# Layer-wide transformer kernel: other PSUM bank counts for head outputs and filling units, and a reordered filling plan

## The chip, the cores and the metric

One Trainium2 chip, one of its cores, one launch. The metric is the device time of a launch in microseconds, here the median of three runs. A profiled execution of the same kernel has its own time, given beside the others below.

## The reference

Two attention layers over a batch of 8 sequences of 512 rows by 512 columns, 16 heads of 32 columns each. All is fp32.

```python
def layer0(tgt, memory, Wq, Wk, Wv):               # x, ctx_1024: (8, 512, 512)
    q, k, v = heads(tgt @ Wq.T), heads(memory @ Wk.T), heads(memory @ Wv.T)
    att = softmax(q k^T / sqrt(32)) v
    return tgt + att[0]                            # sequence 0's attention, added to all eight

def layer1(x, y, ...):                             # x is layer0's result, y is ctx_1024 again
    xq, ykv = layer_norm(x, gq, bq), layer_norm(y, gkv, bkv)
    q = heads(xq @ Wq); k, v = heads(ykv @ Wkv)
    x = x + concat(softmax(q k^T * 32**-0.5) v) @ Wproj + bproj
    h = gelu(layer_norm(x, gm, bm) @ W1 + b1)      # 512 -> 2048, exact gelu
    return x + h @ W2 + b2                         # 2048 -> 512
```

Layer 0's attention is needed for sequence 0 alone. So the kernel runs nine attentions: number 0 is layer 0 on sequence 0, numbers 1 to 8 are layer 1 on the eight sequences.

## The kernel before

**Units and ticks.** Every product is done on a pair of fp32r halves (high, and the remainder, low), three matmuls for a product, so that the result keeps fp32's accuracy. The program is laid out by hand in 621 ticks (class `Plan`, from L46). A tick of an attention holds its core work: one matmul of scores `S` (L925, `ps_s`, for the row maximum), one of scores turned round `t` (L940, `ps_t`, seven ticks later, for the exponentials) and two that weigh values `O` (L908, `ps_o`, nine ticks later). Four ticks make a head, 64 an attention. Around the core lie filling units, which use the banks `ps_d`: `k`, `q`, `v` (projections), `out` (Wproj), `hid` (W1) and `y2` (W2), each 12 matmuls of 512 columns in 4 parts of 3, and the transposes `a` (normed ctx or x), `tg` (layer 0's output) and `ht` (normed h), each 4 transposes of 128x128 in one part.

**Where a unit lands.** `spread` lays a list of units over a run of ticks, evenly by cost (12 for a matmul unit, 2 for a transpose unit). A tick has three places: 0 behind `S`, 1 behind `t`, 2 behind the first `O` pairs; with `front=True` all goes to place 0. PE runs all of it in one order. Attention 0 (ticks 4 to 77) is filled with the projections of sequences 1 to 6 (`early`, `keys_values(b)`), then comes a gap of 8 ticks without core work (`late`, transposes of layer 0's output), then attentions 1 to 8. Attention 1, and the first third of attention 2, are filled with `queries` (units `q` and `a` in turn). Attentions 2 to 8 are filled with the previous sequence's `out`, `ht`, `hid` and `y2` units; the tail (`if tail`) does the last sequence without core work.

**Banks and evacuation.** `bank(u)` (L529) gives unit number i bank i % 3 of `ps_d`, and PE waits before its first matmul until unit i - 3 is evacuated (L820). A unit is evacuated in the order of the plan (`EVACUATED`): for `k`, `q`, `v` ScalarE writes the high half (L955), VectorE the low one (L1109); for `a` and `ht` ScalarE applies gain and bias twice (L959, L960), then VectorE subtracts (L1109); `out`, `y2` and `hid` take one VectorE instruction (L1136, L1146, L1139), `tg` two (L1130, L1131). A unit that ends at place 0 is evacuated behind the tick's row maximum and ahead of its exponentials; one that ends at place 1 behind the tick's exponentials (and, on ScalarE, behind the head's `o_raw` copy); one that ends at place 2 at the next tick's start. ScalarE's and VectorE's queues are in that order too, with the core's exponentials (two a tick, L1054 and L1061), row maxima (L1212), `p_lo` (L1225), norms (L1159, L1016) and inverses (L1174 to L1185) in them.

**Heads' outputs.** The four `O` pairs of a head add up in one bank `ps_o`. ScalarE copies it out (`move_head`, L1005, `o_raw`), and the next head's first `O` waits for that copy (L900).

**Weight pieces.** GpSimd splits W1 and W2 into halves in 16 pieces (`piece`, L1258 and L1260, `piece_tick` at L330), between its own `p_lo` work (L1324). SyncE loads a piece two ticks ahead of it and stores it one tick behind it, in the same queue that loads heads and row maxima.

Of the kernel before, what the change touches and what calls it, by code (L numbers as in the profile page):

```python
# [5 lines left out]
F32 = mybir.dt.float32  # L6
F32R = mybir.dt.float32r
ACT = mybir.ActivationFunctionType
# [3 lines left out]
P = 128  # L12
T = 512
D = 512
F = 2048
B = 8
NH = 16
DK = D // NH
FC = D // P
TC = T // P  # L20
HC = F // P
G = P // DK
# [5 lines left out]
VW = 2 * DK + 1  # L28
# [23 lines left out]
PRE = 4  # L52
# [8 lines left out]
class Plan:  # L61
# [42 lines left out]
    def build(self):  # L104
        spread = self.spread
        for t, units in enumerate(([("k", 0, 0)], [("q", 0, 0)], [("v", 0, 0), ("v", 0, 1)],
                                   [("v", 0, 2), ("v", 0, 3)])):
            spread([t], units, front=True)

        t0 = PRE  # L110
        self.core(0, CH, t0)
        spread(range(t0, t0 + 9), [(kind, 0, g) for g in range(1, G) for kind in "kq"])

        def keys_values(b):
            units = []
            for c in range(4):
                units += [("k", b + 1, c), ("v", b + 1, c)]
                if b + 1 < B:
                    units.append(("a", 3 + b, c))
            return units  # L120

        early = [("a", 2, c) for c in range(FC)]
        for b in range(6):
            early += keys_values(b)
        drained = t0 + CH + WEIGH
        spread(range(t0 + 9, drained), early)
        late = keys_values(6) + keys_values(7)

        gap = drained
        first = [("a", 10, c) for c in range(FC)]  # L130
        for i, units in enumerate(([("tg", 0, g) for g in range(G - 1)] + late[:2], late[2:6], [("tg", 0, G - 1)],
                                   late[6:11], late[11:14],
                                   [u for pair in zip(first, late[14:18]) for u in pair], [("q", 1, 0)],
                                   late[18:] + [("q", 1, 1), ("q", 1, 2)])):
            spread([gap + i], units, front=True)
        self.gap = gap

        self.base = {n: gap + 8 + (n - 1) * CH for n in range(1, NP + 1)}
        self.core(CH, NP * CH, self.base[1])
        queries = [("q", 1, 3)] + [("a", 11, c) for c in range(FC)]  # L140
        for n in range(2, NP):
            for g in range(G):
                queries.append(("q", n, g))
                if n + 1 < NP:
                    queries.append(("a", 10 + n, g))
        base = self.base
        spread(range(base[1], base[2] + 15), queries[:-6])

        def second(n, group):
            return [("y2", n, 4 * group + t) for t in range(TC)]  # L150

        def hidden(n, group):
            return [("hid", n, 4 * group + c) for c in range(4)]

        def burst(tick, n, group, units):
            self.bursts.setdefault(tick, []).append((n, group))
            spread([tick], units, front=True)

        def by_chunk(tick, n, group):
            self.by_chunk.setdefault(tick, []).append((n, group))  # L160

        for n in range(2, NP + 1):
            at, old, new = base[n], n - 2, n - 1
            tail = n == NP
            outs = [("out", new, t) for t in range(TC)]
            turns = [("ht", new, c) for c in range(FC)]
            if tail:
                spread([at + 5], second(old, 1)[:2], front=True)
                spread([at + 6], second(old, 1)[2:], front=True)
                burst(at + 7, old, 2, hidden(old, 3))  # L170
                drain = at + WEIGH
                spread([drain - 1], second(old, 2)[:2], behind=True)
                by_chunk(drain - 1, old, 3)
                spread([drain + 1], second(old, 2)[2:], front=True)
                spread([drain + 2], second(old, 3)[:1], front=True)
                spread([drain + 3], outs, front=True)
                spread([drain + 4], second(old, 3)[1:3], front=True)
                spread([drain + 5], turns[:2] + second(old, 3)[3:] + turns[2:], front=True)
                spread([drain + 6], hidden(new, 0), front=True)
                by_chunk(drain + 6, new, 0)  # L180
                spread([drain + 7], hidden(new, 1), front=True)
                by_chunk(drain + 7, new, 1)
                spread([drain + 8], second(new, 0), front=True)
                spread([drain + 9], hidden(new, 2), front=True)
                by_chunk(drain + 9, new, 2)
                spread([drain + 10], second(new, 1), front=True)
                spread([drain + 11], hidden(new, 3), front=True)
                by_chunk(drain + 11, new, 3)
                spread([drain + 12], second(new, 2), front=True)
                spread([drain + 13], second(new, 3), front=True)  # L190
                self.ticks = drain + 15
                continue
            if old:
                burst(at + 5, old, 2, second(old, 1)[:2])
                spread(range(at + 6, at + 15), second(old, 1)[2:] + hidden(old, 3)[:3])
                spread(range(at + 15, at + 22), outs)
                spread(range(at + 22, at + 24), hidden(old, 3)[3:])
                burst(at + 24, old, 3, second(old, 2)[:2])
                rest = second(old, 2)[2:]
                spread(range(at + 25, at + 40), rest + turns + hidden(new, 0))  # L200
                burst(at + 40, new, 0, second(old, 3)[:2])
                spread(range(at + 41, at + 55), second(old, 3)[2:] + hidden(new, 1))
            else:
                spread(range(at + 15, at + 22), outs)
                spread(range(at + 22, at + 35), queries[-6:])
                spread(range(at + 35, at + 48), turns + hidden(new, 0))
                burst(at + 48, new, 0, hidden(new, 1)[:2])
                spread(range(at + 49, at + 55), hidden(new, 1)[2:])
            burst(at + 55, new, 1, second(new, 0)[:2])
            spread(range(at + 56, at + CH + 5), second(new, 0)[2:] + hidden(new, 2))  # L210
# [5 lines left out]
PLAN = Plan()  # L216
NO = PLAN.no
# [109 lines left out]
PIECES = 16  # L327


def piece_tick(i):  # L330
    return PRE + 19 + 5 * i if i < PIECES // 2 else PLAN.gap - 11 + 2 * (i - PIECES // 2)


PIECE_SPLIT = listed([(piece_tick(i), i) for i in range(PIECES)])
# [88 lines left out]
def xattn_program(nc, x, ctx, x0t, ctx0t, l0wq, l0wk, l0wv, wq, wk, wv, wo, w1, w2, cols, bproj, b2, ident, out):  # L423
# [22 lines left out]
    v_s = sb("v_s", [P, 2, TC, G, VW], F32R)  # L446
# [7 lines left out]
    o_raw = sb("o_raw", [P, 2, T], F32)  # L454
# [68 lines left out]

    ps_s = nc.alloc_psum_tensor("ps_s", [P, 2, T], F32)
    ps_t = nc.alloc_psum_tensor("ps_t", [P, 2, T], F32)
    ps_o = nc.alloc_psum_tensor("ps_o", [P, T], F32)
    ps_d = nc.alloc_psum_tensor("ps_d", [P, 3, T], F32)

    def bank(u):  # L529
        return ps_d[:, NO[u] % 3]  # L530

    sem = nc.alloc_semaphore

# [24 lines left out]
    evacuated = sem("evacuated")  # L558
# [17 lines left out]
    o_moved = sem("o_moved")  # L576
# [235 lines left out]
    def _(pe):  # L812
# [4 lines left out]

        def part(kind, n, c, i):
            u = (kind, n, c)
            if i == 0 and NO[u] >= 3:  # L820
                pe.wait_ge(evacuated, NO[u] - 2)
            if kind == "a":
                if n == 10:
                    src = xt0
                else:
                    src = stage[:, (STAGE_NO["y", n - 2] if n < 10 else STAGE_NO["x", n - 10]) % 2]
# [68 lines left out]
        def values(s):  # L895
            h, c = divmod(s, TC)
            group = h // G
            if c == 0:
                if h:
                    pe.wait_ge(o_moved, h)  # L900
                if h % G == 0:
                    pe.wait_ge(v_loaded[group % 2], 16 * (group // 2 + 1))
            if c in POOL_CHUNKS:
                pe.wait_ge(p_pool_split, by_gpsimd(s))
            else:
                pe.wait_ge(p_split, by_vector(s))
            for m, src in enumerate((p_hi, p_lo)):
                ins = nc.tensor.matmul(ps_o[0:VW], v_s[:, group % 2, c, h % G], src[:, c],  # L908
                                       start=(c == 0 and m == 0), stop=(c == TC - 1 and m == 1))
            ins.then_inc(pv_done, 1)  # L910

# [40 lines left out]
    def _(act):  # L952
# [48 lines left out]
        def move_head(h):  # L1001
            act.wait_ge(pv_done, h * TC + TC)
            if h >= 2:
                act.wait_ge(o_placed[(h - 2) % G], ((h - 2) // G + 1) * (16 * PLACE_DMAS))
            act.activation(o_raw[0:VW, h % 2], ps_o[0:VW], ACT.Identity).then_inc(o_moved, 1)  # L1005

        def scaled(kind, i, t):
            no = NORM_NO[kind, i]
# [26 lines left out]
        for tick in range(TICKS):  # L1035
# [11 lines left out]
            if s is not None:  # L1047
                c = s % TC
# [367 lines left out]
```

## Time and profile before

| | us |
|---|---|
| median of 3 runs | 1790.82 (1788.2 to 1792.63) |
| profiled execution | 1793.32 |
| its span, first to last instruction | 1791.5 |
| PE busy in the span | 1714.7 |
| ACT, DVE, POOL busy | 1156.1, 1082.1, 939.3 |
| mean granted TensorE clock | 0.991 of full speed |

PE is TensorE's matmuls and PEld its weight loads; DVE is VectorE, ACT ScalarE, POOL GpSimd, SP SyncE; a q behind an engine's name is its sequencer, which issues DMAs. Matmuls are pipelined, so PE counts as busy while matmuls follow each other; a wait shorter than a matmul's own latency hardly shows as idle time, and is read from the start times. The profiled execution is 2.5 us (0.14%) above the median of the runs, 1.8 us of it outside the span.

### The profile page before, as it was taken

How to read it: one execution, taken by the hardware profiler on the slowest of the kernel's cores; microseconds unless marked ns; L12 is line 12 of the kernel's file. 1: busy time of each engine (PE TensorE's matmuls, PEld its weight loads, DVE VectorE, ACT ScalarE, POOL GpSimd, SP SyncE). 2: the span in 40 equal slices, each digit the busy share in tenths (PEclk: the TensorE clock that was granted, in tenths of full speed). 3: DMA queues.
4: the chain of work that ended last, by engine and by line, in shares of the span. 5: the costliest groups of instructions: out<-in, count | busy, mean ns of one | idle time of the engine just before them, and what ended most of it. 6: DMA issues, size and time to landing. Idle time of an engine off the chain costs nothing.

```text
span 1791.5 us, 23794 instructions
## 1 busy us (share of the span) xinstructions
PE 1714.7 (96%) x7456; PEld 1313.6 (73%) x7456; DVE 1082.1 (60%) x1865; ACT 1156.1 (65%) x1940; POOL 939.3 (52%) x802
## 2 busy tenths in 40 slices
PE   7899998998989999999999999999999999999999
PEld 5677776765666777777777777777777777777787
DVE  5565654477776666665666665666656666654322
ACT  4777764587877765765766577657657665775231
POOL 0444455157675564656465564646664655646341
PEclk9999999999999999999999999999999999999999
DMA  8789978674545675676676566756766775668262
GB/s 285 251 278 302 330 275 322 229 213 164 188 132 162 184 201 138 179 235 162 160 219 195 143 168 185 200 133 179 235 168 157 219 197 142 171 185 274 93 234 79
DMA packets 160077, 356.78 MB, mean 199 GB/s; under 512 B 29392, under 2 KB 50000, under 8 KB 159312
## 3 DMA queue, kind: packets, MB, share of 16 engines
q1 hardware_dynamic: 109072, 189.31, 35.8%
q10 hardware_dynamic: 50880, 165.95, 29.5%
q8 instruction: 61, 1.00, 0.2%
q14 instruction: 64, 0.52, 0.1%
HBM read 253.61 MB, written 82.08 MB: 187 GB/s over the span
## 4 chain that ended last, share of the span: by engine, by line
PE 69%; ACT 8%; DMA 7%; DVE 5%; issue 4%; POOL 3%; SPq 2%; ACTq 0%; DVEq 0%; POOLq 0%
PE ps_d L887 46%; PE ps_o L908 11%; PE ps_t L940 6%; PE ps_s L925 5%; DMA q_st<-negmax_t 3%; ACT p_hi L1054 2%; DVE negmax L1212 1%; DMA rs<-o_raw 1%; ACT ps_d L960 1%; ACT ps_t L1061 1%; ACT ht L1016 1%; POOL p_lo L1324 1%; SPq L728 1%; PE ps_d L815 1%; DMA v_scratch<-v_out 1%
## 5 line engine op out<-in xcount | busy, mean ns | idle before, releaser
L1324 POOL TENSOR_TENSOR p_lo<-p_full,p_hi 128x512 fp32r<-128x512 f32 x288 | 372.1, 1292 | 586.5 <-ACT p_full L1061 586.0
L1054 ACT ACTIVATE p_hi<-ps_t 128x512 fp32r<-128x512 f32 x576 | 345.7, 600 | 358.5 <-PE ps_t L940 355.0
L1212 DVE TENSOR_REDUCE negmax<-ps_s 128x1 fp32r<-128x512 f32 x576 | 388.9, 679 | 128.2 <-PE ps_s L925 127.6
L887 PE MATMUL ps_d<-hT,w_r 128*128 128x512 f32 x1536 | 419.0, 393 | 2.0 <-DVE hT L1109 2.0
L887 PE MATMUL ps_d<-w_r,g_s 128*128 128x512 f32 x1536 | 389.4, 393 | 0.0
L887 PEld LDWEIGHTS ps_d<-hT,w_r 128*128 128x128 f32 x1536 | 288.6, 189 | 73.7 <-DVE hT L1109 5.7
L887 PEld LDWEIGHTS ps_d<-w_r,g_s 128*128 128x128 f32 x1536 | 290.3, 189 | 64.6
L1225 DVE TENSOR_TENSOR p_lo<-ps_t,p_hi 128x512 fp32r<-128x512 f32 x288 | 198.8, 690 | 229.9 <-ACT ps_t L1061 229.2
L908 PE MATMUL ps_o<-p_hi,v_s 128*65 128x512 f32 x576 | 231.5, 402 | 14.7 <-POOL p_lo L1324 8.1
L940 PE MATMUL ps_t<-q_st,k_st 97*128 97x512 f32 x576 | 232.2, 403 | 11.6 <-DMA q_st<-negmax_t 10.9
L925 PE MATMUL ps_s<-k_st,q_st 96*128 96x512 f32 x576 | 231.8, 402 | 8.4 <-DVE negmax L1212 6.6
L908 PE MATMUL ps_o<-p_lo,v_s 128*65 128x512 f32 x576 | 227.4, 395 | 0.0
L1332 POOL TENSOR_TENSOR g_s<-h_st,g_s 128x512 fp32r<-128x512 f32 x128 | 166.2, 1309 | 74.7 <-ACT g_s L1072 74.6
L1061 ACT ACTIVATE ps_t<-ps_t 128x512 f32<-128x512 f32 x288 | 172.8, 600 | 0.0
L1061 ACT ACTIVATE p_full<-ps_t 128x512 f32<-128x512 f32 x288 | 172.1, 598 | 0.0
L925 PEld LDWEIGHTS ps_s<-k_st,q_st 96*128 96x128 f32 x576 | 109.1, 189 | 55.2 <-DVE negmax L1212 12.6
L940 PEld LDWEIGHTS ps_t<-q_st,k_st 97*128 97x128 f32 x576 | 109.0, 189 | 43.4 <-DMA q_st<-negmax_t 18.8
L1139 DVE TENSOR_SCALAR h_st<-ps_d,col_s 128x512 f32<-128x512 f32 x128 | 94.3, 736 | 43.2 <-PE ps_d L887 42.5
L908 PEld LDWEIGHTS ps_o<-p_hi,v_s 128*65 128x65 f32 x576 | 78.5, 136 | 56.8 <-ACT o_raw L1005 13.1
L887 PE MATMUL ps_d<-aT,wk_s 128*128 128x512 f32 x384 | 107.6, 407 | 8.2 <-DVE aT L1109 6.7
L908 PEld LDWEIGHTS ps_o<-p_lo,v_s 128*65 128x65 f32 x576 | 78.7, 137 | 48.2 <-issue 0.6
L887 PE MATMUL ps_d<-aT,wq_s 128*128 128x512 f32 x384 | 110.9, 402 | 0.0
(102 smaller groups left out, 2160.6 us busy)
## 6 DMA issues: line engine op xcount, KB each, us to landing
w_r<-w_scratch ACTq DMA_DIRECT2D x214, 512.0 KB, 5.3
w_r<-w_scratch SPq DMA_DIRECT2D x42, 512.0 KB, 4.7
v_scratch<-v_out SPq DMA_DIRECT2D x36, 520.0 KB, 5.2
k_scratch<-kq_out SPq DMA_DIRECT2D x36, 512.0 KB, 4.9
q_st<-q_scratch SPq DMA_DIRECT2D x144, 128.0 KB, 4.5
k_st<-k_scratch SPq DMA_DIRECT2D x144, 128.0 KB, 4.3
o_ab<-o_raw SPq DMA_DIRECT2D x144, 128.0 KB, 3.5
w_scratch<-piece_out SPq DMA_DIRECT2D x16, 1024.0 KB, 6.4
```

Source lines behind the costliest of these rows:

```text
L728: sp.dma_start(q_st[KQ:KM, h % G, c * P:c * P + P].bitcast(F32), negmax_t[c:P:32, h % 2]).then_inc(row_loaded[h % 2], 16)
L887: ins = nc.tensor.matmul(bank(u), lhs[a], rhs[b], start=(i == 0 and m == 0), stop=(i == 3 and m == 2))
L908: ins = nc.tensor.matmul(ps_o[0:VW], v_s[:, group % 2, c, h % G], src[:, c], start=(c == 0 and m == 0), stop=(c == TC - 1 and m == 1))
L925: nc.tensor.matmul(ps_s[:, c % 2], q_st[0:KQ, h % G, c * P:c * P + P], k_st[0:KQ, h % G], start=True, stop=True).then_inc(s_ready, 1)
L940: nc.tensor.matmul(ps_t[:, c % 2], k_st[0:KM, h % G, c * P:c * P + P], q_st[0:KM, h % G], start=True, stop=True).then_inc(t_ready, 1)
L1054: act.activation(p_hi[:, c], ps_t[:, c % 2], ACT.Exp, scale=SCALE)
L1061: act.activation(whole, ps_t[:, c % 2], ACT.Exp, scale=SCALE).then_inc(p_exp, 1)
L1139: dve.tensor_scalar(hidden_of(n, c // 4)[:, c % 4], bank(u), col_s[:, 6 * FC + c:6 * FC + c + 1], None, ALU.add).then_inc(evacuated, 1)
L1212: dve.tensor_reduce(negmax[:, h % 2, c:c + 1], ps_s[:, c % 2], AX.X, ALU.max, negate=True).then_inc(s_maxed, 1)
L1225: dve.tensor_tensor(p_lo[:, c], ps_t[:, c % 2], p_hi[:, c].bitcast(F32), ALU.subtract).then_inc(p_split, 1)
L1324: pool.tensor_tensor(p_lo[:, c], p_full[:, (by_gpsimd(s) - 1) % 2], p_hi[:, c].bitcast(F32), ALU.subtract).then_inc(p_pool_split, 1)
L1332: pool.tensor_tensor(g_s[:, done % 2, 1, c], hidden_of(n, group)[:, c], g_s[:, done % 2, 0, c].bitcast(F32), ALU.subtract).then_inc(g_lo, 1)
```

## The change

Five edits. The two PSUM ones go together, since PSUM has eight banks and the kernel uses all of them.

- `ps_o` has two banks, used by heads in turn; a head's first `O` waits for the copy of the head before the previous one. `ps_d` has two banks in place of three; a unit waits for the evacuation of the unit two before it.
- `keys_values`: the order of a sequence's units. Before: k0 v0 a0 k1 v1 a1 k2 v2 a2 k3 v3 a3. After: k0 v0 a0 k1 a1 v1 a2 k2 a3 v2 k3 v3 (`a` of the next sequence). The lists `early` and `late` are made of it, the latter cut at the same places.
- Attentions 3 to 8: the last two `y2` units of group 2 get ticks 25 to 27 of the attention for themselves, and the `ht` and `hid` units behind them ticks 28 to 39; before, all shared ticks 25 to 39.
- Tail: the last `y2` unit of the seventh sequence's group 3 comes ahead of the four `ht` units; before, it stood behind the second of them.
- W2's pieces (8 to 15) come six ticks earlier: ticks 60, 62, ... 74 in place of 66 to 80.

```diff
         def keys_values(b):
             units = []
-            for c in range(4):
-                units += [("k", b + 1, c), ("v", b + 1, c)]
-                if b + 1 < B:
-                    units.append(("a", 3 + b, c))
+            turns = [("a", 3 + b, c) for c in range(FC) if b + 1 < B]
+            units = [("k", b + 1, 0), ("v", b + 1, 0), *turns[:1], ("k", b + 1, 1), *turns[1:2], ("v", b + 1, 1), *turns[2:3],
+                     ("k", b + 1, 2), *turns[3:], ("v", b + 1, 2), ("k", b + 1, 3), ("v", b + 1, 3)]
             return units
...
-                spread([drain + 4], second(old, 3)[1:3], front=True)
-                spread([drain + 5], turns[:2] + second(old, 3)[3:] + turns[2:], front=True)
+                spread([drain + 4], second(old, 3)[1:], front=True)
+                spread([drain + 5], turns, front=True)
...
-                spread(range(at + 25, at + 40), rest + turns + hidden(new, 0))
+                spread(range(at + 25, at + 28), rest)
+                spread(range(at + 28, at + 40), turns + hidden(new, 0))
...
 def piece_tick(i):
-    return PRE + 19 + 5 * i if i < PIECES // 2 else PLAN.gap - 11 + 2 * (i - PIECES // 2)
+    return PRE + 19 + 5 * i if i < PIECES // 2 else PLAN.gap - 17 + 2 * (i - PIECES // 2)
...
-    ps_o = nc.alloc_psum_tensor("ps_o", [P, T], F32)
-    ps_d = nc.alloc_psum_tensor("ps_d", [P, 3, T], F32)
+    ps_o = nc.alloc_psum_tensor("ps_o", [P, 2, T], F32)
+    ps_d = nc.alloc_psum_tensor("ps_d", [P, 2, T], F32)
 
     def bank(u):
-        return ps_d[:, NO[u] % 3]
+        return ps_d[:, NO[u] % 2]
...
-            if i == 0 and NO[u] >= 3:
-                pe.wait_ge(evacuated, NO[u] - 2)
+            if i == 0 and NO[u] >= 2:
+                pe.wait_ge(evacuated, NO[u] - 1)
...
             if c == 0:
-                if h:
-                    pe.wait_ge(o_moved, h)
+                if h >= 2:
+                    pe.wait_ge(o_moved, h - 1)
...
-                ins = nc.tensor.matmul(ps_o[0:VW], v_s[:, group % 2, c, h % G], src[:, c],
+                ins = nc.tensor.matmul(ps_o[0:VW, h % 2], v_s[:, group % 2, c, h % G], src[:, c],
...
-            act.activation(o_raw[0:VW, h % 2], ps_o[0:VW], ACT.Identity).then_inc(o_moved, 1)
+            act.activation(o_raw[0:VW, h % 2], ps_o[0:VW, h % 2], ACT.Identity).then_inc(o_moved, 1)
```

## Rows read from the trace of the kernel before

**Rows 1.** The page: shares of the span of the chain that ended last, by engine.
```profile
PE 69%; ACT 8%; DMA 7%; DVE 5%; issue 4%; POOL 3%; SPq 2%; ACTq 0%; DVEq 0%; POOLq 0%
```

**Rows 2.** Busy time by stretch: stretch, length, engines with instruction counts, clock, DMA, GB/s.
```profile
130.00:200.00 70.00, 68.19 (x312) 53.48 (x311) 48.56 (x88) 50.20 (x88) 36.84 (x32) 1.00 0.96 319
...
343.00:420.00 77.00, 64.23 (x280) 45.31 (x278) 54.54 (x104) 60.84 (x107) 43.54 (x45) 0.98 0.67 215
420.00:490.00 70.00, 64.49 (x273) 46.39 (x274) 52.06 (x97) 58.87 (x108) 41.39 (x39) 0.95 0.54 174
490.00:560.00 70.00, 64.43 (x281) 46.71 (x279) 49.69 (x93) 52.15 (x96) 43.70 (x42) 1.00 0.38 121
641.00:806.00 165.00, 162.63 (x707) 124.42 (x706) 103.59 (x176) 110.84 (x186) 93.25 (x76) 1.00 0.64 180
```

**Rows 3.** The waits, whole span: who waited for whom, total us, times, longest.
```profile
PEld ps_o L908 <- ACT o_raw L1005: 13.1, 28, 1.3
...
PE ps_o L908 <- ACT o_raw L1005: 4.1, 8, 0.9
```

**Rows 4.** Timeline, attention 0, first v-a-k: start, length, engine, line, what, [idle before].
```profile
72.53 0.84 PE L887 MATMUL ps_d<-wv_s,aT 128*128 128x512 f32 x3
...
73.45 0.60 PE L815 MATMUL ps_d<-id_s,stage 128*128 128x128 f32 x4
73.47 0.65 ACT L955 ACTIVATE v_out<-ps_d 128x512 fp32r<-128x512 f32 x1 [2.21 <-PE ps_d L887]
...
73.81 1.63 PE L887 MATMUL ps_d<-aT,wk_s 128*128 128x512 f32 x6
...
74.16 0.69 DVE L1109 TENSOR_TENSOR v_out<-ps_d,v_out 128x512 fp32r<-128x512 f32 x1 [0.73 <-ACT v_out L955]
```

**Rows 5.** Timeline, attention 0, one of its last v-a-k.
```profile
245.70 0.94 PE L887 MATMUL ps_d<-aT,wk_s 128*128 128x512 f32 x3
...
246.30 0.69 DVE L1109 TENSOR_TENSOR v_out<-ps_d,v_out 128x512 fp32r<-128x512 f32 x1 [0.34 <-ACT v_out L955]
```

**Rows 6.** Timeline, the gap: ScalarE's norm, the last transpose's evacuation, PE.
```profile
305.55 1.50 ACT L1016 ACTIVATE xt<-xt,shift,rstd 128x512 f32<-128x512 f32 x2
...
306.95 0.76 ACT L959 ACTIVATE aT<-ps_d,col_s 128x512 fp32r<-128x512 f32 x1
...
309.37 1.65 PE L887 MATMUL ps_d<-aT,wk_s 128*128 128x512 f32 x3 [3.36 <-DVE aT L1109]
```

**Rows 7.** Timeline, PE near attention 0's end.
```profile
262.00 0.42 PE L908 MATMUL ps_o<-p_hi,v_s 128*65 128x512 f32 x1 [2.27 <-POOL p_lo L1324]
```

**Rows 8.** Timeline, attention 1, first q-a-q.
```profile
358.72 0.69 DVE L1109 TENSOR_TENSOR kq_out<-ps_d,kq_out 128x512 fp32r<-128x512 f32 x1 [0.43 <-ACT kq_out L955]
358.74 0.86 PE L887 MATMUL ps_d<-aT,wq_s 128*128 128x512 f32 x3
```

**Rows 9.** Timeline, attention 3, from the last y2 unit to hid.
```profile
719.16 0.85 PE L887 MATMUL ps_d<-w_r,g_s 128*128 128x512 f32 x3
...
720.09 0.60 PE L815 MATMUL ps_d<-id_s,ht 128*128 128x128 f32 x4
...
722.82 0.68 DVE L1146 TENSOR_TENSOR xres_b<-ps_d,xres_b 128x512 f32<-128x512 f32 x1
...
723.55 0.66 PE L815 MATMUL ps_d<-id_s,ht 128*128 128x128 f32 x4 [1.25 <-DVE xres_b L1146]
```

**Rows 10.** Timeline, tail: the last four transpose units.
```profile
1693.61 1.31 PE L815 MATMUL ps_d<-id_s,ht 128*128 128x128 f32 x8 [3.05 <-ACT ht L1016]
...
1694.57 4.45 PE L887 MATMUL ps_d<-w_r,g_s 128*128 128x512 f32 x12
```

**Rows 11.** Busy time by stretch, around falls of the clock (columns as in rows 2).
```profile
308.50:315.30 6.80, 5.93 (x14) 4.67 (x15) 1.51 (x3) 0.60 (x1) 0.00 (x0) 0.50 0.41 165
421.10:424.50 3.40, 3.40 (x9) 2.42 (x8) 2.04 (x4) 2.72 (x5) 1.27 (x1) 0.50 0.72 233
411.70:421.10 9.40, 6.74 (x27) 4.38 (x28) 5.31 (x10) 6.38 (x12) 8.38 (x11) 1.00 0.48 175
```

## The prediction

> **What bounds the kernel now.** Read first the shares of the chain that ended last: PE holds 69% of it, and no other engine more than 8% [rows 1]. So the kernel is priced in PE's time, and what matters elsewhere is what makes PE wait. Then the busy times by stretch: in attention 0 and in the steady attentions PE is busy 97 to 99% of the time, 68.2 of 70 us and 162.6 of 165 us; in attention 1 and the start of attention 2 it idles 12.8, 5.5 and 5.6 us, 24 us in all [rows 2]. So a new wait on PE adds whole in the first kind of stretch, and in the second it can take the place of waits that are there. Then the waits: the copy of a head's output holds PE up 4.1 us in 8 places, and its weight loads 13.1 us in 28 [rows 3]. Last the timeline, at the places where a fourth unit now finds a third bank and will not after the change.
>
> **Two banks in place of three, attention 0.** A unit must then wait until the unit two before it is evacuated. Between them lies one unit. Where that is 12 matmuls, it is about 2.8 us of PE (a part of three takes 0.7 us by its start times), and the cover is enough. Where it is a transpose unit, its four transposes take 0.36 us: from 73.45 to the next part at 73.81 [rows 4]. The evacuation of a `v` is ScalarE's 0.65 us and, behind it, VectorE's 0.69 us, and the trace has its end at 74.85; the `k` two units on starts at 73.81 [rows 4]. In the changed kernel both have one bank, and PE waits the 1.04 us. One of the last such triples: end 246.99, start 245.70, short by 1.29 us [rows 5]. Attention 0 has 23 such triples v-a-k, and each is short, by 0.27 to 1.83 us, 1.07 us on average. The new order of `keys_values` doesn't take them away. It makes them, in each sequence, v0-a0-k1, k1-a1-v1, v1-a2-k2 and k2-a3-v2: four for four. A `k` is evacuated by the same two instructions as a `v`. So 6 sequences x 4 x 1.07 = **+25.7 us**. The four transpose units in a row at its start already wait for banks; with one bank fewer I estimate +2.5 (0 to 4). The bounds of the 25.7 are 17, if every evacuation ran at its shortest with no work ahead of it in the queues, and 31.
>
> **The new order's gain.** What it does remove is the wait of the next sequence's first `k` for the last transpose unit. In the gap ScalarE has two more norm instructions ahead of that evacuation (1.50 us), it starts at 306.95, and PE idles 3.36 us [rows 6]; the clock then stands at 0.50 for 6.8 us [rows 11], in which half the work is lost, 3.4 us. After the change two to three units lie between, at 2.8 us each. **-6.8 us** in the gap, and -3.0 for two smaller cases of the kind in attention 0.
>
> **The gap's own bank waits.** Eight triples with an `a` in the middle remain there, with no core work to lengthen them: 1.25 us each, the size of the second one above [rows 5], and 0.8 of it waited already: **+9.5**. The transposes of layer 0's output wait for banks before and after; I put nothing. The gap comes to +2.7, with -1 to +10 as bounds.
>
> **Pieces six ticks earlier.** GpSimd's pieces near the end of attention 0 make its `p_lo` late, and PE waits 2.27 us for one [rows 7]. In SyncE's queue each piece's load and store now pass six ticks of heads, row maxima and stores, in a stretch just behind one with a DMA share of 0.96 [rows 2]. The same crowding can come six ticks sooner, so I take -1.5 out of -3 to +2.
>
> **Attentions 1 and 2: q-a-q.** A `q` ends its evacuation at 359.41, and the `q` two units on starts at 358.74: short by 0.67 us [rows 8]. Of 23 such triples 19 are short, by 0.2 to 3.7 us, 20.5 us in all; the long ones are those that end behind the tick's exponentials. With four `a` in a row at the head (+2) and the first `ht` (+2) that is 24.5 us. But here PE idles 24 us already, some 17 of it for row maxima, GpSimd and DMA, work that goes on while PE waits for a bank. I take half of the 17 as absorbed: **+16.5**, between 8 (all of it) and 24 (none).
>
> **Heads' outputs.** The wait that the second bank removes is 4.1 us by PE's idle time, and at most 13.1 by its weight loads', which overlap matmuls [rows 3]. **-5**, being nearer to the idle time.
>
> The Trainium skill, Perfetto Trace Analysis, section Matmuls, asks that independent groups of matmuls rotate through different banks so that one's evacuation overlaps the next one's matmuls. It holds for both rotations alike, and by it the change would only gain: the first rival below. The rows agree with it for groups of 12 matmuls alone, and not for those of four transposes.
>
> **ht units, six steady attentions.** Before, PE idles 1.25 us at the third `ht`, which waits for the last `y2` unit's addition: that ends at 723.50, and the transposes start at 723.55 [rows 9]. The new ticks bring that `y2` unit's end ahead of the first `ht` by a tick's core work, but with two banks the second `ht` needs it, and its addition is still queued behind the next row maximum: 1.2 us. The fourth `ht` needs the second one's evacuation, which on ScalarE stands behind two exponentials and an `o_raw` copy, 1.8 us, then takes two instructions of about 0.75 (one such in [rows 6]) and VectorE's 0.7: about 4.1 us, against 1.6 us of PE work between: 2.5. The third `ht` and the first `hid` add 0.6. That is 4.3 against 1.25, so +3.0, six times **+18** (9 to 25).
>
> **Tail.** PE idles 3.05 us ahead of the first `ht`, and the 12 matmuls of the `y2` unit stand behind it and take 4.45 us where 12 otherwise take 2.8 [rows 10]. Moved ahead, they fill the idle time. But the four `ht` units then have nothing between them and two banks: each from the second on waits for the `y2` unit's or an earlier `ht`'s evacuation, 0.5, 2, 1.3 and, for the first `hid`, 1.3 us. I put **0** (-2 to +3).
>
> **Clock.** It fell to half for 3.4 us behind a stretch of 9.4 us with PE busy for 6.74 [rows 11]. New waits of 1 us every 3 to 8 us are sparser than that, but in attention 1 they join waits that are there. I add two to three falls of 1.7 us each: **+4** (0 to 15).
>
> **Sum.** 25.7 + 2.5 - 3.0 + 2.7 - 1.5 + 16.5 - 5 + 18 + 0 + 4 = +59.9. The profiled execution would go from 1793.3 to 1853.2; it stands 2.5 us above the median of the runs, and the sum is put on that: 1790.8 + 60 = **1851 us**, 3.3% slower. The low ends of the terms together give +12, the high ends +107; they are independent enough that I take 1815 to 1890 for this case.
>
> **Rivals.**
> - *The waits are covered, and the kernel is faster.* If evacuations kept ahead of PE with two banks, the gains would stand alone: 13.1 at most for heads' outputs, 9.8 for the order, 3 for pieces and 3 in the tail: 1790.8 - 29 = 1762, or about 1775 with half of them. It decides at about 25 us of bank waits: below that the change is faster. Against it speak the ends and starts in rows 4, 5 and 8, of instructions that need one bank after the change. 4%; no difference, 2%.
> - *Half is absorbed everywhere.* PE's waits let ScalarE's and VectorE's queues run dry, so evacuations come at their shortest, and core waits vanish: 17 + 0 + 8 + 9 less the gains of 15 or so gives +20: 1811. For it: PE's idle time in attention 1 [rows 2]. Against it: PE has next to no idle time elsewhere. 14%.
> - *The clock.* Waits join to stretches like that in rows 11, and 20 more falls come, most in attentions 0 and 1: 20 x 1.7 = 34 in place of 4: 1881. For it: one fall in attention 1 came from small waits alone. Against it: in attention 0 most new waits stand alone. 10%.
>
> **Chances.** The forecast 70%, the others as above. A measurement of this kernel can tell about 0.3%, 5.4 us, from no change: faster 0.04, the same 0.02, slower 0.94. The range, which holds what lies between the second rival and the third, is 1815 to 1890.
>
> **What would show it.** In the profile after: PE waits at L887 and L815 for L1109, about 1 us each, in some 24 places in attention 0 and 8 in the gap; four small waits at the `ht` units of each steady attention in place of one; none at `ps_o` for `o_raw`; no wait of 3.36 us in the gap. A steady attention would grow from 164 us by about 3. It would be wrong if the waits for L1109 summed to under 30 us, or if another engine's work behind these waits came later than I count it.

## The result, and the profile after

The change makes the kernel slower: 1858.4 us against 1791.7, a ratio of 1.035 (95% interval 1.033 to 1.037), +63 us by the ratio. The span of the profiled execution goes from 1791.5 to 1855.7 us. The forecast was 1851, +60.

The waits of PE in the changed kernel, whole span (who waited for whom: total us, times, longest):

```profile
PE ps_d L887 <- DVE kq_out L1109: 32.8, 30, 3.6
PE ps_d L887 <- DVE v_out L1109: 18.8, 17, 2.5
PE ps_d L815 <- DVE hT L1109: 17.3, 15, 1.9
PE ps_d L815 <- DVE kq_out L1109: 9.2, 3, 7.2
...
PE ps_o L908 <- POOL p_lo L1324: 1.6, 2, 0.9
```

Four rows of waits for banks hold 78 us. The row of heads' outputs waiting for `o_raw`, 4.1 us of PE's idle time before [rows 3], is gone from the list. All four were ended by the low half's instruction on VectorE (L1109), the last step of an evacuation.

Busy time by stretch, for the stretches that answer to [rows 2], and two in which the clock stood at half (columns: length, then PE, PEld, DVE, ACT, POOL, each with its instruction count, granted clock, DMA share, GB/s):

```profile
130.00:200.00 70.00, 61.91 (x277) 47.14 (x276) 41.62 (x77) 45.19 (x79) 29.91 (x27) 1.00 0.78 259
376.00:453.00 77.00, 61.74 (x258) 45.34 (x258) 53.82 (x101) 56.70 (x99) 38.99 (x41) 0.92 0.64 201
453.00:528.00 75.00, 67.49 (x293) 48.86 (x293) 53.99 (x100) 63.82 (x115) 45.89 (x44) 0.97 0.56 176
682.00:850.00 168.00, 164.95 (x707) 126.34 (x707) 104.71 (x176) 111.27 (x186) 93.30 (x76) 0.98 0.64 178
764.40:771.20 6.80, 5.64 (x15) 4.00 (x16) 4.35 (x8) 5.62 (x10) 5.05 (x4) 0.50 0.58 200
...
61.20:74.80 13.60, 9.19 (x26) 6.62 (x27) 4.06 (x6) 10.27 (x16) 6.24 (x5) 0.50 0.10 43
```

In the same 70 us of attention 0 PE starts 277 matmuls where it started 312 [rows 2]; a steady attention's 707 matmuls take 168 us where they took 165. In attention 0 the clock is full in that stretch, so what is missing there is waits alone. In the steady attention the clock has fallen to half for 6.8 us, which it didn't do before.

The first v-a-k triple of the changed kernel, on the timeline (start, length, engine, line, operation, tiles, idle time before), answers to [rows 4]:

```profile
79.76 0.84 PE L887 MATMUL ps_d<-wv_s,aT 128*128 128x512 f32 x3
...
80.67 0.60 PE L815 MATMUL ps_d<-id_s,stage 128*128 128x128 f32 x4
80.70 0.64 ACT L955 ACTIVATE v_out<-ps_d 128x512 fp32r<-128x512 f32 x1 [2.20 <-PE ps_d L887]
...
81.37 0.69 DVE L1109 TENSOR_TENSOR v_out<-ps_d,v_out 128x512 fp32r<-128x512 f32 x1 [0.72 <-ACT v_out L955]
...
82.11 1.20 PE L887 MATMUL ps_d<-aT,wk_s 128*128 128x512 f32 x4 [0.84 <-DVE v_out L1109]
```

The transposes start at 80.67 and the `k` could follow 0.36 us later, at 81.03; the `v` unit's evacuation ends at 82.06 and the `k` starts at 82.11. The engines' own durations are as before. The idle time shown, 0.84, is shorter than the loss by start times, 1.08, since the last transpose still counts as busy.

Stretch by stretch, from the start times of PE's matmuls, in us. A matmul at full clock counts 0.231 and a transpose 0.109, their usual distance from start to start; what the falls of the clock cost is at most that much again for each one that starts in them; the waits at units are those ahead of a unit's first instruction; the rest is core waits and waits inside a unit, such as the 3.36 us of [rows 6].

| stretch | forecast | longer by | waits at units | clock | rest |
|---|---|---|---|---|---|
| start and attention 0 | +23.7 | +30.0 | +37.8 | +3.8 | -11.5 |
| gap | +2.7 | +2.6 | +8.3 | -2.8 | -2.9 |
| attentions 1 and 2 | +11.5 | +8.4 | +25.3 | +3.6 | -20.5 |
| attentions 3 to 8 | +18 | +22.3 | +12.9 | +11.4 | -2.0 |
| tail | 0 | +0.8 | +0.7 | +1.2 | -1.1 |
| clock, all | +4 | | | +17.2 | |
| sum | +59.9 | +64.1 | +85.0 | +17.2 | -38.1 |

The same start times say which units wait. Where 12 matmuls stand between a unit and the one two before it, 5 of 394 units start more than 0.3 us late, and all 394 together 7.7 us; in the kernel before it was 4, and 7.4 us. Where four transposes stand between, 84 of 100 do, 109.5 us together; before it was 17, and 25.8 us. So nearly all the new waits at units are behind transpose units.

### The profile page after: what moved, and what is told of

It reads as the page before. It is cut to its first block, busy times and chain, and to the rows that moved or that the text cites. A ratio compares the mean times of both kernels' runs of the same rounds, so it can differ in the third digit from the quotient of the medians.

```text
span 1855.7 us, 23794 instructions
## 1 busy us (share of the span) xinstructions
PE 1736.8 (94%) x7456; PEld 1329.2 (72%) x7456; DVE 1088.8 (59%) x1865; ACT 1160.4 (63%) x1940; POOL 939.3 (51%) x802
## 4 chain that ended last, share of the span: by engine, by line
PE 75%; DVE 7%; DMA 6%; ACT 5%; issue 2%; SPq 2%; POOL 2%; DVEq 0%; ACTq 0%; POOLq 0%
PE ps_d L887 51%; PE ps_o L908 12%; PE ps_t L940 6%; PE ps_s L925 6%; DMA q_st<-negmax_t 2%; DMA rs<-o_raw 2%; DVE negmax L1212 1%; DVE kq_out L1109 1%; DVE stats L1159 1%; SPq L728 1%; ACT ps_d L960 1%; ACT p_hi L1054 1%; SPq L723 1%; ACT ps_t L1061 1%; PE ps_d L815 1%
## 5 line engine op out<-in xcount | busy, mean ns | idle before, releaser
L887 PE MATMUL ps_d<-hT,w_r 128*128 128x512 f32 x1536 | 427.9, 399 | 2.2 <-DVE hT L1109 2.0
L887 PEld LDWEIGHTS ps_d<-hT,w_r 128*128 128x128 f32 x1536 | 294.7, 192 | 76.9 <-DVE hT L1109 6.5
L887 PE MATMUL ps_d<-aT,wq_s 128*128 128x512 f32 x384 | 115.0, 414 | 21.0 <-DVE kq_out L1109 19.7
L887 PE MATMUL ps_d<-wv_s,aT 128*128 128x512 f32 x384 | 103.4, 396 | 13.3 <-DVE kq_out L1109 13.1
```

The source lines that it names most:

```text
L887: ins = nc.tensor.matmul(bank(u), lhs[a], rhs[b], start=(i == 0 and m == 0), stop=(i == 3 and m == 2))
```

## The experiments

The theory: PE waits for banks behind units of four transposes, because an evacuation lasts longer than they do, and with two banks nothing else lies between. The rivals: the moved work costs the time; the clock does; the evacuating engines' rate does. Times are differences by the ratio to the kernel before on the same chip, with the ratio's interval.

**The order edits without the PSUM edits.** The changed kernel with

```diff
-    ps_o = nc.alloc_psum_tensor("ps_o", [P, 2, T], F32)
-    ps_d = nc.alloc_psum_tensor("ps_d", [P, 2, T], F32)
+    ps_o = nc.alloc_psum_tensor("ps_o", [P, T], F32)
+    ps_d = nc.alloc_psum_tensor("ps_d", [P, 3, T], F32)
...
-                pe.wait_ge(evacuated, NO[u] - 1)
+                pe.wait_ge(evacuated, NO[u] - 2)
...
-                    pe.wait_ge(o_moved, h - 1)
+                    pe.wait_ge(o_moved, h)
```

> All of the change but the PSUM edits: the new order of the filling units, the new ticks for ht, the new tail, the early pieces, with one bank for heads' outputs and three for the units as before. My theory, that the time is lost to bank waits behind transpose units: without them the order's gains stand alone, 6.8 in the gap, 3 in attention 0, 1.5 for pieces, up to 3 in the tail, so about 1791 - 12 = 1779 us. The rival, that the moved work itself costs the time (the transposes in a row in the tail, the pieces beside more DMAs, the ht ticks): 1815 us or more.

Measured: +2.1 us (-0.9 to +5.0), 1794.7. The moved work does not cost the time: the first rival is out. But the gain of 12 isn't there either. The waits of PE in this kernel say where part of it went:

```profile
PE ps_d L887 <- DVE hT L1109: 9.0, 9, 1.4
...
PE ps_d L815 <- ACT stage L1016: 4.6, 3, 3.3
...
PE ps_d L815 <- DVE hT L1109: 3.8, 7, 1.4
```

The steady attentions are 8.7 us longer than before (waits behind the `ht` units in more places, three falls of the clock), and the transposes `a` of sequence 7 wait 3.3 us for their norm. The gap is 4.3 us shorter and the tail 2.7.

**The PSUM edits without the order edits.** The kernel before with

```diff
-    ps_o = nc.alloc_psum_tensor("ps_o", [P, T], F32)
-    ps_d = nc.alloc_psum_tensor("ps_d", [P, 3, T], F32)
+    ps_o = nc.alloc_psum_tensor("ps_o", [P, 2, T], F32)
+    ps_d = nc.alloc_psum_tensor("ps_d", [P, 2, T], F32)
...
-                pe.wait_ge(evacuated, NO[u] - 2)
+                pe.wait_ge(evacuated, NO[u] - 1)
...
-                    pe.wait_ge(o_moved, h)
+                    pe.wait_ge(o_moved, h - 1)
```

> The PSUM edits alone on the kernel before: two banks for heads' outputs, two for the units, the old order. My theory: the whole cost of the change and none of its order's gain, 1858 + 10 = about 1868 us, with waits for evacuations at the k behind each transpose unit, and with waits for a last transpose unit still there. The rival, that the order costs the time: within 10 us of the kernel before.

Measured: +65 us (61 to 70), 1859.9. This is the whole cost, in the old order. The order's gain of 10 is missing here as well: 1859.9 against 1858.4. In the profiles the new order has the shorter gap and tail, by 4.5 and 4.3 us, and the longer attention 0 and attentions 3 to 8, by 6.6 and 3.2.

**The wait alone, with three banks there.**

```diff
-                pe.wait_ge(evacuated, NO[u] - 2)
+                pe.wait_ge(evacuated, NO[u] - 1)
```

> The kernel before with nothing changed but the wait: each unit waits for the evacuation of the unit two before it, as if there were two banks; three are there, and heads' outputs have one. Beside the kernel with the PSUM edits alone in the old order this prices the second bank for heads' outputs. My theory: 5 us slower than that one (between 4 and 13), about 1873 us. The rival, that waits for banks take the place of the waits for o_raw: the same within 2 us, since PE's other waits give the copy its time.

Measured: +67 us (64 to 71), 1861.5. Nothing else differs from the kernel before, so a wait for the evacuation of the unit two before is enough to make the loss. The second bank for heads' outputs is worth 1.6 us beside it, within what these runs can tell from nothing, and not 5. The rival of this run came out: where PE waits for banks, the copy has its time anyway; the row of waits for `o_raw` is gone from this kernel's list too, with one bank.

**The a units' transposes twice, in the changed kernel.**

```diff
-            for t in range(TC):
+            for t in [*range(TC)] * (2 if u[0] == "a" else 1):
```

> The changed kernel with the four transposes of each of the 64 units a done twice into the same bank: 256 more transposes of about 0.11 us, 28 us more of PE's work. My theory, that PE waits behind these units because they are too short to cover an evacuation: the work goes into waits that are there already, and the time rises by less than 8 us, or falls if fewer falls of the clock come: 1850 to 1866 us. The rival, that the evacuations' own rate sets the waits (a longer unit only ends later, and so does its evacuation): 1858 + 28 = 1886 us.

Measured: +56 us (51 to 61), 1852.1: 6 us faster than the changed kernel, with 256 transposes more. Its waits:

```profile
PE ps_d L887 <- DVE kq_out L1109: 19.0, 23, 3.1
PE ps_d L815 <- DVE hT L1109: 17.3, 15, 1.9
PE ps_d L887 <- DVE v_out L1109: 12.9, 15, 2.5
```

The waits for `k`, `q` and `v` units fall from 32.8 and 18.8 us to 19.0 and 12.9, and those at `ht` units, which were left as they were, stay at 17.3. From a unit `a`'s first transpose to the next matmul, without a wait, PE now takes 0.79 us in the median, where it took 0.36: 64 x 0.43 = 27.6 us of work. By start times the waits at units fall by 25.2 us. So the work goes into the waits, as the theory has it. Had the evacuating engines' rate set the waits, they would have moved along with the longer units, and the time would have grown by 28.

**The same doubling in the kernel before.** The same line.

> The kernel before with the four transposes of each of the 64 units a done twice: the same 256 extra transposes as in the changed kernel with doubled transposes, which became 6 us faster by them. My theory: here there are few waits for them to fill, so 28 us of work, less what attention 1's idle time takes up, +20 (14 to 28), about 1813 us. The rival, that a doubled transpose costs PE little in any kernel (then the other run showed nothing): under +8 us.

Measured: +5.4 us (1.8 to 9.1), 1800.0. This expectation missed, and the rival's number came out, though not for its reason: the transposes take their 0.43 us each here too. By start times the core's waits fall by 15.8 us, the clock's falls by 3.3 and waits at units by 3.2. So the kernel before had some 16 us of core waits that other work can fill, 5 of them in attention 0, where I had counted on none. The two runs differ in where the work goes: in the changed kernel waits at units fall by 25.2 us and the rest by some 4, here by 3.2 and 15.8.

**The wait in one stretch at a time.** The kernel before with the stricter wait under a condition on the tick at which a unit starts:

```diff
-                pe.wait_ge(evacuated, NO[u] - 2)
+                pe.wait_ge(evacuated, NO[u] - (1 if PLAN.starts[u] < PLAN.gap else 2))
```

> The kernel before, three banks and its old order, with the stricter wait (the unit two before) only for units that start in attention 0 and ahead of it. It prices the term of attention 0 alone. My theory: 24 triples of about 1.07 us, 2.5 for the transposes in a row, and nothing to absorb it: +26 us (23 to 31), about 1819 us. The rival, that half is absorbed everywhere: +13, about 1806 us.

Measured: +20 us (13 to 28), 1815.7. Attention 0 itself, without the four ticks ahead of it, is 23.8 us longer in the profile, its waits at units 31 longer and its core waits 10 shorter. By the runs it lies halfway between the two theories; the profile shows why: my price of the waits, and an absorption that I had not expected.

For attention 1 and the start of attention 2:

```diff
+                pe.wait_ge(evacuated, NO[u] - (1 if PLAN.base[1] <= PLAN.starts[u] < PLAN.base[2] + 48 else 2))
```

> The kernel before with the stricter wait only for units that start in attention 1 and the first 48 ticks of attention 2. My theory: bank waits of some 24 us, of which the waits for row maxima, GpSimd and DMAs that were there before take up half: +12 us (8 to 16), about 1805 us. The rivals: nothing absorbed, +24; all taken up, 0 to +4, which is also what it would be if these stretches were bound by another engine.

Measured: +7.7 us (3.4 to 12), 1800.2. The waits for `q` units alone are as in the changed kernel; this kernel's row first, then the changed kernel's from 376 to 682 us, attentions 1 and 2:

```profile
PE ps_d L887 <- DVE kq_out L1109: 19.3, 16, 3.6
...
PE ps_d L887 <- DVE kq_out L1109: 19.7, 16, 3.6
```

By start times the waits at units grow by 25.0 us, and the core waits fall from 30.9 to 9.4 us. So more than three quarters are taken up, not half, by waits that were there already.

For attentions 3 to 8:

```diff
+                pe.wait_ge(evacuated, NO[u] - (1 if PLAN.base[3] <= PLAN.starts[u] < PLAN.base[9] else 2))
```

> The kernel before with the stricter wait only for units that start in attentions 3 to 8. My theory: 12 to 14 us of waits at the ht units, and one or two falls of the clock for 3.4 us in each of the six attentions, 1.7 us each: +20 us, about 1813 us, with the clock at 0.5 once in each attention. The rival, waits alone and no falls of the clock: +12, about 1805 us.

Measured: +21 us (14 to 28), 1816.1. In the profile the six attentions are 20.0 us longer, 13.0 of it waits at units and 10.1 the clock, which falls once in each attention, and in none before. The rival without falls of the clock is out. The three stretches make 20 + 7.7 + 21 = 49 of the 67 us of the wait everywhere; the gap and the tail, 8.7 and 5.8 us longer there, make up the rest within the intervals.

**The ht units' transposes twice, in the changed kernel.**

```diff
-            for t in range(TC):
+            for t in [*range(TC)] * (2 if u[0] == "ht" else 1):
```

> The changed kernel with the four transposes of each of the 32 ht units done twice: 128 more transposes, 14 us of PE's work by their 0.11 us each. My theory, that PE waits there because these units are too short, and that the waits bring the clock's fall in each steady attention: the work goes into the waits, and falls go: -5 to +3 us against the changed kernel, 1853 to 1861 us, with fewer falls after 682 us. The rival, that ScalarE's rate sets the end of the whole group of ht units: the waits stay, in number and size less than 0.3 us shorter each, and so do the falls; still no more than +5 us. The third, that the work adds: +14.

Measured: +61 us (58 to 65), 1852.8, 5.6 us less than the changed kernel. The stretch of attentions 3 to 8 in the changed kernel, and in this one:

```profile
682.00:1690.00 1008.00, 985.55 (x4228) 755.08 (x4228) 626.56 (x1056) 666.65 (x1106) 559.96 (x457) 0.98 0.65 177
```

```profile
680.00:1687.00 1007.00, 984.66 (x4318) 757.81 (x4317) 624.92 (x1055) 665.32 (x1104) 559.81 (x456) 1.00 0.62 176
```

With 96 transposes more in attentions 3 to 8 the stretch is as long, and the clock 1.00 in place of 0.98. The clock's cost there falls from 11.4 to 1.5 us: one fall where there had been six. The waits at units shrink by 3.9 us only, and core waits grow by 3.7, so of the 10.5 us of work the clock pays nearly all. So the falls hang on what PE does at these units; the second rival's forecast that the falls would stay is out, its forecast that the waits would nearly stay came out. That waits shrank by less than the work says that ScalarE's order of work sets the end of this group in part.

**Which of the order edits is worth keeping.** The kernel before with the new `keys_values`, as in the change, and the new tail alone:

```diff
-                spread([drain + 4], second(old, 3)[1:3], front=True)
-                spread([drain + 5], turns[:2] + second(old, 3)[3:] + turns[2:], front=True)
+                spread([drain + 4], second(old, 3)[1:], front=True)
+                spread([drain + 5], turns, front=True)
```

> The kernel before, with its banks, and of the change only the new order of projections and transposes and the new tail; not the early pieces, not the new ht ticks. My theory now: the run with all order edits came out even because the new order and the tail gain some 7 us (gap 4, tail 3) and the other two edits lose them again. So this one gains 7 us (3 to 10): about 1785 us, better than both kernels. The rival, that the gains are not there in unprofiled runs or go into other waits: the same within 3 us.

Measured: -4.7 us (-7.3 to -2.0), 1788.5: 0.26% faster than the kernel before, and so faster than both. Attention 0 is 2.7 us shorter in its profile, the tail 1.9, the gap 0.7.

The early pieces alone, in `piece_tick`:

```diff
-... PLAN.gap - 11 + 2 * (i - PIECES // 2)
+... PLAN.gap - 17 + 2 * (i - PIECES // 2)
```

> The kernel before with the early pieces alone. My theory: the wait for GpSimd near the end of attention 0 only moves, and the last transposes of attention 0 wait for a norm whose GpSimd steps stand behind a piece, 3.5 us: 0 to +4 us in attention 0, nothing elsewhere. The rival, as in my prediction: -1.5 us, and -3 at best.

Measured: +3.2 us (0.4 to 6.1), 1796.2. The longest wait for GpSimd's `p_lo` is 3.6 us there, where it was 2.3 [rows 7]: it moved and grew. The norm's wait that I named is 0.7 us in this kernel, so the 3.3 us above needs the new order too; what makes it I did not settle.

The new `ht` ticks alone:

```diff
-                spread(range(at + 25, at + 40), rest + turns + hidden(new, 0))
+                spread(range(at + 25, at + 28), rest)
+                spread(range(at + 28, at + 40), turns + hidden(new, 0))
```

> The kernel before with the new ticks for the y2, ht and hid units of the steady attentions alone, three banks. My theory: in place of one wait of 1.5 us there are two to four smaller ones, together 2.3 us, at the fourth ht and in the first hid, which now follow each other more closely than ScalarE evacuates them: +5 us over six attentions (1 to 9, with falls of the clock). The rival, that the split frees the transposes from the y2 unit's addition and does no more: -9 us.

Measured: +9.1 us (6.1 to 12.2), 1800.2. The wait for the `y2` unit's addition [rows 9] is gone, and waits for `hT` take its place:

```profile
PE ps_d L888 <- DVE hT L1110: 8.6, 9, 1.3
...
PE ps_d L816 <- DVE hT L1110: 2.4, 6, 0.4
```

In the profile the six attentions are 4.6 us longer, 3.0 of it the clock, so the profile shows half of the 9.1.

## Why the prediction was right, point by point

The mechanism, an evacuation that outlasts four transposes, is the one that the runs show, at the units named. That the sum came within 4 us is in part luck: the clock cost 13 us more than its term, and the other terms together 9 us less.

**Attention 0's triples.** 24 of 1.07 us were forecast, 25.7 in all. In the changed kernel 23 such waits of over 0.3 us add up to 26.8 us from start to start, 1.17 each. The price was read from ends and starts that would need one bank after the change, and the run with the wait alone shows that nothing else is needed.

**The transposes in a row at its start** were put at +2.5 and cost more. On the timeline:

```profile
60.32 1.91 ACT L1101 ACTIVATE wv_s<-whole_raw 128x2048 fp32r<-128x2048 f32 x1 [3.85 <-DMA whole_raw<-wv]
62.13 0.58 ACT L955 ACTIVATE kq_out<-ps_d 128x512 fp32r<-128x512 f32 x1
...
62.75 0.69 DVE L1109 TENSOR_TENSOR kq_out<-ps_d,kq_out 128x512 fp32r<-128x512 f32 x1 [3.83 <-ACT kq_out L955]
...
63.49 1.11 PE L815 MATMUL ps_d<-id_s,stage 128*128 128x128 f32 x4 [7.22 <-DVE kq_out L1109]
```

The `q` unit's evacuation stands on ScalarE behind a weight's high half, which waits 3.85 us for its load. With three banks PE didn't need it so soon. 7.2 us of idle time go by, and the clock falls in them, at 61.2, for 13.6 us. The step had priced the evacuation by its own instructions and left out what is ahead of it in the queue. Part of the 7.2 is this execution's: in the profiles of four other runs with the stricter wait (everywhere, in attention 0, in the old order, and with `ht` doubled) the load is waited for 0.6 to 1.4 us, and these transposes wait 4.4 to 4.9 us by start times, against 7.4 here. In the kernel before ScalarE has no wait there.

**What took it back in attention 0.** I wrote that a new wait adds whole there. It doesn't: the rest is 11.5 us shorter in the changed kernel, and 10 in the run with the wait in attention 0 alone. Of the 11.5, 5.7 us are core waits in its first nine ticks, well ahead of the 70 us that I had read as full [rows 2], 3.1 are core waits at `O`, the 2.27 us for GpSimd's `p_lo` [rows 7] among them, and 2.1 are waits inside units. Order and pieces were to take 4.5. So 10 us of waits too few and 7 of absorption too few cancel in part, and the clock's 3.8 us make up the 6.3 by which this stretch missed.

**The order's gain** of 9.8 us came where its wait was read and was lost elsewhere. The wait of 3.36 us in the gap [rows 6] is gone, and with it 2.9 us of waits inside units, and 2.1 more in attention 0; the clock gives back 2.8 us in the gap where 3.4 were put. But other units wait now: in the run with the order edits and three banks a `v` unit in the gap waits for the transposes, 1.7 and 1.4 us by start times, and with the order and the tail alone 5.3 and 1.4, since the order brings them closer to it (at the 5.3 their low half stands on VectorE behind an inverse that waits 4.36 us for its DMA); the gap gained 4.3 us in the one and 0.7 in the other. As a gain in time this was the step that failed: with two banks the order is worth 1.5 us by the runs. The price of the wait that goes was read; what is late next was not looked for.

**The pieces** were put at -1.5 and cost 3.2 us alone (0.4 to 6.1).

**The gap** came out as put, +2.6 for +2.7, and its parts nearly so: 8.3 us of bank waits for 9.5 (eight of 1.25 less 0.8 would be 9.2), -2.8 of the clock for -3.4, and -2.9 of the rest, which is the wait of 3.36 us.

**q-a-q.** 24.5 us of bank waits were forecast for attentions 1 and 2, and they grew by 25.3. Half of 17 us of core waits was to be absorbed; 20.5 us of the rest went. So the term of 16.5 was 8 to 10, and that of heads' outputs, -5, was -1.6 by the two runs on it, within their noise.

**ht units.** The timeline in attention 3 of the changed kernel:

```profile
760.74 0.68 DVE L1146 TENSOR_TENSOR xres_b<-ps_d,xres_b 128x512 f32<-128x512 f32 x1
...
761.47 0.66 PE L815 MATMUL ps_d<-id_s,ht 128*128 128x128 f32 x4 [0.70 <-DVE xres_b L1146]
...
762.77 0.66 PE L815 MATMUL ps_d<-id_s,ht 128*128 128x128 f32 x4 [0.40 <-DVE hT L1109]
762.90 0.59 ACT L1005 ACTIVATE o_raw<-ps_o 65x512 f32<-65x512 f32 x1
...
764.82 0.69 DVE L1109 TENSOR_TENSOR hT<-ps_d,hT 128x512 fp32r<-128x512 f32 x1 [1.10 <-ACT ps_d L960]
...
765.56 0.69 PE L815 MATMUL ps_d<-id_s,ht 128*128 128x128 f32 x2 [1.90 <-DVE hT L1109]
```

The three waits are the ones named, for the `y2` unit's addition, for the first and for the second `ht`'s evacuation behind the exponentials and `o_raw`; 0.70, 0.40 and 1.90 us where 1.2, 0.3 and 2.5 were put. Over the six attentions waits make 12.9 us of the 18, and the clock, which I had not put there, another 11.4.

**The clock** was the term most mis-sized: +4 forecast, +17.2 measured. I took single waits of 1 us as too sparse to bring a fall. But the three waits at the `ht` units, 3.0 us together, stand between 760 and 766 us, and the clock fell at 764.4, in the third; in each of the other five attentions it fell in that wait or up to 1.6 us behind it. The third rival had the mechanism, for attentions 0 and 1 and at 34 us.

**Tail.** The idle time ahead of the first `ht` went, and waits of 1.76, 0.68 and 0.44 us between the units took its place, where 0.5, 2, 1.3 and 1.3 were put: +0.8 in all.

The Trainium skill, Perfetto Trace Analysis, section Matmuls, asks for groups that rotate through different banks so that one's evacuation overlaps the next one's matmuls. With two banks the changed kernel's trace agrees for groups of 12 matmuls (5 of 394 units behind one are late) and not for four transposes (84 of 100), whose 0.36 us an evacuation of 1.3 us outlasts.

## What to carry to other kernels

A ring of banks is measured by the shortest unit in it: list, for each unit, the end of the evacuation that it would wait for with one bank fewer and its own start in the trace of the present kernel, and sum the negative differences by stretch; that sum came out within some 1 us in attention 0's triples, in the gap and in attentions 1 and 2, and not where a load stood ahead of the evacuation. Then ask what else PE waits for in the stretch, since those waits shrink, and what stands ahead of each evacuation in its engine's queue. A bank is better spent where PE waits for it most, here 4 us at the heads' outputs against some 80 at the units.

## What the runs showed of the hardware that I had not expected

Short waits close together can bring the clock down: in the changed kernel's steady attentions three waits, 0.70, 0.40 and 1.90 us in attention 3, went with 3.4 or 6.8 us at 0.50 from the third one on, once in each attention, and none of these waits is longer than 2.2 us by start times. 96 transposes put there kept it at 1.00 but for one fall, and cost no time. In attention 1, falls vary between executions of the same work: in the kernel before and six others whose attention 1 does the same they cost 1.4 to 7.0 us (4.5 in the kernel before), so a difference of that size in one profile, such as the table's +3.6, is no finding.
